# Head attention on one core: PSUM banks dealt out as two for the output and three fixed pairs, in place of one and a pool of seven

## The chip, the cores and the metric

The kernel runs on one core of a Trainium2 chip. The metric is the device time of one launch in microseconds (us); the three runs of the kernel before took 1464.88, 1465.10 and 1467.75 us, a median of 1465.1. TensorE has its own queue (PE, its weight loads shown as PEld), VectorE is DVE, ScalarE is ACT, GpSimd is POOL, and SP issues transfers. PSUM has eight banks of 128 partitions by 512 floats, and a matmul of 512 columns fills one bank.

## The reference, cut to what matters

One layer: layer norm, then a causal attention and a second attention with 16 heads over the same rows, then a routed feed-forward. The change lies in the second attention:

```python
attn = jnp.einsum('bhqd,bhkd->bhqk', q, k) / np.sqrt(DH)   # B=4, H=16, S=1024, DH=16
attn = jax.nn.softmax(attn, axis=-1)
sa = jnp.einsum('bhqk,bhkd->bhqd', attn, v)
```

The kernel takes the largest score of each query row first, subtracts it inside the score matmul, and lets ScalarE make the exponentials. The sums of the rows come out of the output matmul, whose values carry columns of ones.

## The kernel before, in words

The function `head_attention` works through 16 **steps** (4 batches by 4 groups of 4 heads). A step is cut into 16 **units**: two halves `c` of 512 queries, times eight blocks `j` of 128 keys. A unit has two **turns**, one for each pair of heads; I count turns through the whole stage as h = 0, 1, 2 and so on, so a step has 32 turns, unit u has the turns 2u (even) and 2u+1 (odd), and the last turn is 511. TensorE's program for one turn is, in this order:

- **scores** (`score`, L1687): two matmuls of 512 columns, one for each head of the pair, into the pair of banks `PAIR` of this turn; their increment `scored` releases ScalarE.
- **turned maxima** (`turn_maxima`, L1676), once a step: the finished maxima are transposed into one bank.
- **item** (`item`, L1668): two matmuls of 512 columns that compute scores again, of a later turn's step, for the maxima alone. They go into the pair of banks `SLOT`. The items run 40 turns ahead, so in the steady part each turn has one, and from turn 472 on there is none.
- **mix** (`mix`, L1708): half of the unit before's output matmuls, probabilities times values, 256 queries wide, added up in the bank `po` over the eight key blocks of a half `c`. The last block of a half `c` is not split: nothing in the even turn, all 512 columns in the odd turn.

ScalarE makes two exponentials for each scores pair (`fill`, L1768), in the order of the turns; `exp_done` counts them. Before the first exponential of a unit it also waits until the probabilities' buffer is free (`pv_done`). After four exponentials into the next half `c` it copies the finished output out of PSUM (`take_out`, L1775), which `out_taken` counts, and stores it. VectorE makes one reduction over both banks of an item (`maximum`, L1799); `sq_free` counts these and the readings of the turned maxima.

Each engine runs its own program in order, so a wait holds back all that stands behind it on the same engine. What TensorE waits for before it may write to a bank is worked out when the program is built: `Banks.give` notes who held each bank last, and `emptied` waits for all exponentials and reductions among these holders. The wait stands at the first weight load of the two matmuls and covers both banks. The banks come from the tables `PAIR_BANKS` and `SLOT_BANKS`, which repeat every seven turns. From the tables, and from the order of the program, follows for the steady part:

- scores of turn h wait, in five turns of seven, for the second exponential of turn h-2 and for the reduction of the item of turn h-2; in the sixth for that reduction alone, and in the seventh for the second exponential of turn h-2 and the first of turn h-1;
- the item of turn h waits, in five turns of seven, for the reduction of the item of turn h-2 and for the **first** exponential of turn h-1; in the sixth for the first exponential of turn h-1 alone, and in the seventh for the reduction of turn h-2 alone.

The output bank `po` is one. The first mix of a half `c` therefore waits for `take_out` of the half before:

```python
if j == 0:
    pe.wait_ge(out_taken, n * NQ + c)
```

In the last step (turns 480 to 511) there are no items; two of the seven banks then serve the first chunk of the feed-forward, and the scores go round the other five.

Of the kernel before, what the change touches and what calls it, by code (L numbers as in the profile page):

```python
# [6 lines left out]
F32 = mybir.dt.float32  # L7
BF16 = mybir.dt.bfloat16
F32R = mybir.dt.float32r
ACT = mybir.ActivationFunctionType  # L10
# [3 lines left out]
P = 128  # L14
B, S, D = 4, 1024, 256
N = B * S
CH = 512
# [6 lines left out]
VW = 2 * DH  # L24
# [25 lines left out]
DOTS = NT * DH  # L50
# [34 lines left out]
class HeadInputs:  # L85
# [3 lines left out]
    RING = 3  # L89
# [130 lines left out]
def project(nc, sem, x, w_kv_t, w_q, w_kc, w_vc, w_k, w_v, rope_cos, rope_sin,  # L220
# [7 lines left out]
    with ExitStack() as ctx:  # L228
# [25 lines left out]
        T, KA, VA, Q, KVC, K, V = range(7)  # L254
        BANKS = {T: 0, KVC: 1, KA: 2, VA: 3, Q: 0, K: 1, V: 2}

# [39 lines left out]
        with nc.Block() as block:  # L296
# [84 lines left out]
            def _(act):  # L381
# [11 lines left out]
                def take(it, s, j):  # L393

                    dst, src, stored = {
                        T: (xnT[s][:, :, :], ps[BANKS[T]][:, :, :], "xnT"),
                        KA: (kaT[s][:, :, :], ps[BANKS[KA]][:, :, :], "kaT"),
                        VA: (va[s][:, :, :].rearrange("p j d -> p (j d)"),
                             ps[BANKS[VA]][:, :, :].rearrange("p a b -> p (a b)"), "va"),
                        Q: (qk[:, 0:KD, :], ps[BANKS[Q]][:, :, :], None),  # L400
                        KVC: (kvc[s][:, :], ps[BANKS[KVC]][:, 0, :], None),
                        K: (qk[:, KD:2 * KD, :], ps[BANKS[K]][:, :, :], None),
# [1033 lines left out]
def head_attention(nc, inputs, ot_d, ffw, chunk, routing):  # L1436
# [3 lines left out]
    with ExitStack() as ctx:  # L1440
# [3 lines left out]
        RING = HeadInputs.RING  # L1444
# [3 lines left out]
        NQ = S // CH  # L1448
# [3 lines left out]
        PER = ITEMS // UNITS  # L1452
        PARTS = PAIRS
        assert PER == PARTS
        BANKS = 7
        LEAD = 4
        HELD = PER
        WARM = 8
# [4 lines left out]
        q6, k6, vh = inputs.q6, inputs.k6, inputs.vh  # L1463
        x1p = routing.parts_at(place)
        probs = [sb(f"h_p{i}", [P, GH, CH]) for i in range(PR)]
        outT = [sb(f"h_o{i}", [P, CH]) for i in range(NQ)]
# [4 lines left out]
        negm = room.take(TILES)  # L1471
        mparts = sb("h_mparts", [TILES, SHIFT, P], F32R)
        banks = ctx.enter_context(nc.psum_tensor("h_banks", [P, BANKS, CH], F32))
        po = ctx.enter_context(nc.psum_tensor("h_po", [P, CH], F32))

        const_set = sem("h_const_set")
        ones_set = sem("h_ones_set")
# [5 lines left out]
        out_taken = sem("h_out_taken")  # L1483
# [23 lines left out]
        def item_slot(n, m):  # L1507
            return n * ITEMS + m + max(0, n - 1 + (n >= 1 and m >= HELD))

        def turn_slot(n):  # L1510
            return (n + 1) * ITEMS + n + (HELD if n + 1 < STEPS else 0)

        LAST = STEPS - 1

        PAIR_BANKS = ((0, 1), (4, 0), (1, 2), (5, 6), (2, 3), (6, 0), (3, 4))
        SLOT_BANKS = ((2, 3), (5, 6), (3, 4), (0, 1), (4, 5), (1, 2), (5, 6))
        given = Banks()
        for slot in range(turn_slot(0) + LEAD * PER - HELD + 1):
            given.give(("SLOT", slot), *(SLOT_BANKS[3 + slot % 2] if slot != turn_slot(0) else (6,)))
        for h in range(LAST * UNITS * PARTS):  # L1520
            given.give(("PAIR", h), *PAIR_BANKS[h % BANKS])
            n, m = divmod(h + ITEMS + LEAD * PER, ITEMS)
            if m == HELD and n <= STEPS:
                given.give(("SLOT", turn_slot(n - 1)), PAIR_BANKS[(h + 1) % BANKS][0])
            if n < STEPS:
                given.give(("SLOT", item_slot(n, m)), *SLOT_BANKS[h % BANKS])
        given.give(("FIRST", 0), *OF_FIRST)
        for h in range(LAST * UNITS * PARTS, STEPS * UNITS * PARTS):
            given.give(("PAIR", h), *(b % OF_FIRST.start for b in (h * SIDES, h * SIDES + 1)))
# [5 lines left out]
        def bank_of(key, i=0):  # L1535
            return banks[:, given.places[key][i], :]
# [8 lines left out]
        with nc.Block() as block:  # L1545
# [105 lines left out]
            def _(pe):  # L1651
# [39 lines left out]
                def mix(n, w, part):  # L1691


                    c, j = divmod(w, QT)
                    u, last = n * UNITS + w, j == QT - 1 or n == LAST
                    if part == 0:
                        if j == 0:
                            pe.wait_ge(out_taken, n * NQ + c)
                        if w == 0 and n >= AHEAD:
                            pe.wait_ge(spread, n - AHEAD + 1)  # L1700
                        if last:
                            return
                    if part == 0 or last:
                        pe.wait_ge(exp_done, (u + 1) * GH)
                    at = slice(0, CH) if last else slice(part * CH // PARTS, (part + 1) * CH // PARTS)

                    for h in range(GH):
                        ins = nc.tensor.matmul(po[h * VW:(h + 1) * VW, at], vh[n % RING][:, j, h, :],  # L1708
                                               probs[u % PR][:, h, at], start=j == 0 and (part == 0 or last), stop=j == QT - 1)
                    if part == PARTS - 1:  # L1710
                        ins.then_inc(pv_done, 1)
# [12 lines left out]
                        routing.rank_tokens(pe, 0, first)  # L1724

                def keep_busy():
                    nc.tensor.matmul(po[:, :], q6[0][0:DOTS, 0, 0:P], k6[0][0:DOTS, 0, 0:CH], start=True, stop=True)

                for m in range(ITEMS):
                    item(0, m)  # L1730
                    if m >= ITEMS // 2:
                        keep_busy()
                for m in range(HELD):
                    item(1, m)
                    keep_busy()
                pe.wait_ge(const_set, 2)
                turn_maxima(0)
                for m in range(HELD, LEAD * PER):
                    item(1, m)
                    keep_busy()  # L1740
                for i in range(WARM):
                    nc.tensor.matmul(po[:, :], k6[1][:, 0, 0:P], k6[1][:, 0, 0:CH], start=True, stop=True)
                for u in range(STEPS * UNITS + 1):
                    n, w = divmod(u, UNITS)
                    ahead = [divmod(u * PER + ITEMS + LEAD * PER + b, ITEMS) for b in range(PER)]
# [15 lines left out]
            @block.scalar  # L1761
            def _(act):
                def fill(f):
                    u, h = divmod(f, GH)
                    if h == 0 and u >= PR:
                        act.wait_ge(pv_done, u - PR + 1)
                    act.wait_ge(scored, f // SIDES + 1)
                    nc.scalar.activation(probs[u % PR][:, h, :], bank_of(("PAIR", f // SIDES), f % SIDES), ACT.Exp,  # L1768
                                         scale=DH ** -0.5).then_inc(exp_done, 1)

                def take_out(n, c):
                    act.wait_ge(pv_done, n * UNITS + (c + 1) * QT)
                    if n:
                        act.wait_ge(stored[c], n * 16)
                    nc.scalar.activation(outT[c][:, :], po[:, :], ACT.Copy).then_inc(out_taken, 1)  # L1775

                def store(n, c):
                    act.wait_ge(out_taken, n * NQ + c + 1)
                    act.dma_start(ot_d[n, :, c * CH:(c + 1) * CH], outT[c][:, :]).then_inc(stored[c], 16)

                TAKE = GH
                HALF = QT * GH
                for f in range(STEPS * FILLS + TAKE + 1):
                    if f < STEPS * FILLS:
                        fill(f)
                    if f == LAST * FILLS + ROOT_AT * GH:
                        routing.root_by_log(act)
                    if f == LAST * FILLS + EXP_AT * GH:
                        routing.exponentials(act, 0)
                    if f >= HALF and (f - TAKE + 1) % HALF == 0:  # L1790
                        take_out(*divmod((f - TAKE + 1) // HALF - 1, NQ))
                    if f > HALF and (f - TAKE) % HALF == 0:
                        store(*divmod((f - TAKE) // HALF - 1, NQ))
# [541 lines left out]
def layer(nc, x, w_kv_t, w_q, w_kc, w_vc, w_k, w_v, w_o, ws_in, ws_out, w1, w2, w_g, w_e, b_g, b_e, n1_w, n2_w,  # L2335
# [16 lines left out]
    with ExitStack() as ctx:  # L2352
        heads = HeadInputs(nc, ctx, q_d, k_d, vh_d)
        with ExitStack() as first_stages:
            sem = first_stages.enter_context(stage_semaphores(nc))
            causal = CausalInputs(nc, first_stages, sem, xnT_d, kaT_d, va_d, tokens)
            turning = Turning(nc, first_stages, sem, heads, q_d, k_d)
            project(nc, sem, tokens, w_kv_t, w_q, w_kc, w_vc, w_k, w_v, rope_cos, rope_sin,
                    xn_d, xnT_d, kaT_d, va_d, vh_d, causal, turning)
            causal_attention(nc, sem, causal, xn_d, ya_d, heads, turning)  # L2360
        ffw = FeedForwardWeights(nc, ctx, w_o, ws_in, ws_out, w1, w2, w_g, w_e, b_g, b_e, n1_w, n2_w)
        chunk = Chunk(nc, ctx, ot_d, xn_d, rt_d)
        routing = Routing(nc, ctx, heads, ffw, chunk, idx_d)
        head_attention(nc, heads, ot_d, ffw, chunk, routing)
        feed_forward(nc, chunk, heads, ya_d, ffw, routing, rows_d, hidden_d, out.rearrange("b s d -> (b s) d"))
# [38 lines left out]
```

## Time and profile before

| | |
|---|---|
| median of three runs | 1465.1 us |
| the profiled execution | 1463.6 us |
| its span, first to last instruction | 1461.9 us |
| granted TensorE clock, mean over the span | 0.972 |
| TensorE matmul busy | 1380.3 us, 94% |
| VectorE busy | 1136.0 us, 78% |
| ScalarE busy | 854.8 us, 58% |
| reductions of items, L1799, 512 of them | 617.8 us, 1221 ns each |
| exponentials, L1768, 1024 of them | 551.2 us, 598 ns each |
| copies out, L1775, 32 of them | 598 ns each (median) |

The head attention's interleaved part runs from 345.5 us (first scores) to about 958 us (the start of the last step), and the last step to 1002 us. Shares of the whole span mix this with the stages around it, so the stage is read by its own stretches. A row of the timeline merges instructions of one line on one engine that follow each other; in brackets stands the idle time before them and what ended it. Matmuls are pipelined: the start of a weight load is a firmer mark than the end of a matmul.

### The profile page before, as it was taken

What the parts mean: (1) busy time and instruction counts of PE and PEld (TensorE: products, weight loads), DVE (VectorE), ACT (ScalarE), POOL (GpSimd) and SP (SyncE); (2) the same over time, 40 slices, a digit from 0 to 9 for tenths busy, and PEclk for the clock granted to TensorE, in tenths of its full rate; (3) what the DMA queues carried; (4) which work ended last, traced back from release to release, by engine and by line L of the source; (5) the groups of instructions that cost most, each with busy time, mean ns of one, the idle gap of its engine ahead of it and who ended that gap; (6) DMA issues with size and microseconds to landing.
All of it is one profiled execution on the core that took longest, in us unless ns stands there. A gap on an engine that the chain in (4) does not pass through costs nothing. (4 is left out here: it accounts for less than half of the span.)

```text
span 1461.9 us, 26960 instructions
## 1 busy us (share of the span) xinstructions
PE 1380.3 (94%) x9749; PEld 816.1 (56%) x9749; DVE 1136.0 (78%) x1803; ACT 854.8 (58%) x1573; POOL 371.9 (25%) x368
## 2 busy tenths in 40 slices
PE   6999799979999999999999999989999999989995
PEld 3655577734333333333333333335888888789985
DVE  3786575588999999999999999924677776657764
ACT  2445443304888888888888888885334343323332
POOL 0344294045241000000000000101233333355553
PEclk9999999957999999999999999999999999999998
DMA  5799769351443344443322234213565654365551
GB/s 188 266 320 342 250 224 249 71 98 59 91 109 67 44 67 66 67 67 60 67 55 51 46 58 67 75 59 47 166 161 153 175 152 132 88 217 177 176 174 62
DMA packets 119746, 185.06 MB, mean 127 GB/s; under 512 B 26614, under 2 KB 74122, under 8 KB 119622
## 3 DMA queue, kind: packets, MB, share of 16 engines
q1 hardware_dynamic: 94341, 124.55, 34.6%
q0 software_dynamic: 14816, 45.19, 10.4%
q10 hardware_dynamic: 10464, 13.64, 3.1%
q8 instruction: 82, 1.34, 0.4%
q14 instruction: 43, 0.34, 0.1%
HBM read 102.36 MB, written 81.88 MB: 126 GB/s over the span
## 5 line engine op out<-in xcount | busy, mean ns | idle before, releaser
L1799 DVE TENSOR_REDUCE i_saT<-h_banks 128x2 f32<-128x1024 f32 x512 | 617.8, 1221 | 24.9 <-PE h_banks L1668 17.1
L1768 ACT ACTIVATE h_p<-h_banks 128x512 f32<-128x512 f32 x1024 | 551.2, 598 | 137.3 <-PE h_banks L1687 121.9
L1708 PE MATMUL h_po<-h_p,h_v 128*32 128x256 f32 (+1 forms) x3728 | 318.4, 413 | 3.5 <-ACT h_p L1768 1.4
L1687 PE MATMUL h_banks<-h_q,h_k 50*128 50x512 f32 x1024 | 254.4, 495 | 11.7 <-ACT h_p L1768 6.0
L1668 PE MATMUL h_banks<-h_k,h_q 48*128 48x512 f32 x1024 | 222.8, 431 | 10.7 <-DVE i_saT L1799 6.8
L1687 PEld LDWEIGHTS h_banks<-h_q,h_k 50*128 50x128 f32 x1024 | 95.8, 183 | 235.0 <-ACT h_p L1768 190.4
L1708 PEld LDWEIGHTS h_po<-h_p,h_v 128*32 128x32 f32 x3728 | 73.4, 108 | 170.7 <-issue 83.8
L2130 PE MATMUL f_ob<-w_experts,f_h 128*128 x1032 | 146.4, 291 | 1.3 <-issue 0.2
L2130 PEld LDWEIGHTS f_ob<-w_experts,f_h 128*128 128x128 f32 x1032 | 129.9, 191 | 10.3 <-issue 8.1
L1564 POOL COPY h_v<-h_values 128x512 f32<-128x512 f32 x14 | 8.6, 612 | 459.4 <-DMA h_values<-vh_d 459.4
L1668 PEld LDWEIGHTS h_banks<-h_k,h_q 48*128 48x128 f32 x1024 | 101.1, 194 | 38.4 <-DVE i_saT L1799 28.0
L2176 ACT ACTIVATE h_v<-f_pair 128x512 f32<-128x512 f32 x64 | 38.2, 597 | 131.2 <-PE f_pair L2079 131.1
L2079 PE MATMUL f_pair<-w_routed,r_x1p 128*128 128x512 f32 x384 | 93.7, 400 | 2.1 <-PEq L70 2.1
L2079 PE MATMUL f_pair<-r_x1p,w_shared 128*128 128x512 f32 x384 | 92.9, 396 | 2.3 <-DVE f_rows L2238 2.3
L2079 PEld LDWEIGHTS f_pair<-w_routed,r_x1p 128*128 128x128 f32 x384 | 72.6, 191 | 18.3 <-issue 3.0
L2079 PEld LDWEIGHTS f_pair<-r_x1p,w_shared 128*128 128x128 f32 x384 | 71.3, 187 | 19.8 <-DVE f_rows L2238 3.1
L2238 DVE TENSOR_TENSOR h_place<-h_v,f_pair 128x512 f32<-128x512 f32 x48 | 32.9, 686 | 50.1 <-ACT h_v L2176 49.8
L746 PE MATMUL a_sc<-c_kT,c_qT 128*128 128x512 f32 (+3 forms) x192 | 68.3, 493 | 2.3 <-PEq L296 2.3
L1950 POOL TENSOR_TENSOR f_h<-h_place,f_h 128x512 fp32r<-128x512 f32 x32 | 43.8, 1368 | 98.6 <-ACT f_h L2169 97.0
L2251 DVE TENSOR_TENSOR f_h<-f_pair,f_h 128x512 fp32r<-128x512 f32 x43 | 29.7, 692 | 49.0 <-ACT f_h L2182 49.0
L308 POOL TENSOR_TENSOR h_spare<-h_spare,t_sin 128x512 f32<-128x512 f32 x28 | 41.9, 1530 | 101.3 <-DVE h_spare L184 101.3
L773 PE MATMUL a_out<-a_v,a_pT 128*128 128x256 f32 x432 | 63.6, 298 | 0.0
(266 smaller groups left out, 1695.5 us busy)
## 6 DMA issues: line engine op xcount, KB each, us to landing
h_q<-q_d SPq DMA_DIRECT2D x84, 128.0 KB, 5.9
h_k<-k_d SPq DMA_DIRECT2D x84, 128.0 KB, 7.0
ot_d<-h_o ACTq DMA_DIRECT2D x32, 256.0 KB, 2.9
q_d<-t_parts SPq DMA_DIRECT2D x12, 512.0 KB, 5.0
k_d<-t_parts SPq DMA_DIRECT2D x12, 512.0 KB, 5.1
p_xin<-in_L_attn_x SPq DMA_DIRECT2D x8, 512.0 KB, 5.1
xn_d<-p_xn SPq DMA_DIRECT2D x8, 512.0 KB, 5.1
xnT_d<-p_xnT SPq DMA_DIRECT2D x8, 512.0 KB, 6.0
```

The costliest lines, as they stand in the source:

```text
L308: last = nc.gpsimd.tensor_tensor(swap[:, j, :], swap[:, j, :], sin[:, s, :], ALU.mult)
L746: ins = nc.tensor.matmul(sc[u % 2][:, c:c + w], qT[b % 2][:, k, i * P:(i + 1) * P], kT[b % 2][:, k, c:c + w], start=k == 0, stop=k == KD - 1)
L773: ins = nc.tensor.matmul(out[u % 2][:, 0:D], pT[u % 2][left][:, j, :], vp[b % 2][right][:, j, :], start=j == 0 and n == 0, stop=j == i and ...
L1668: ins = nc.tensor.matmul(bank_of(("SLOT", slot), g), q6[r][at, p, i * P:(i + 1) * P], k6[r][at, p, half * CH:(half + 1) * CH], start=True, ...
L1687: ins = nc.tensor.matmul(bank_of(key, g), k6[r][at, p, j * P:(j + 1) * P], q6[r][at, p, c * CH:(c + 1) * CH], start=True, stop=True)
L1708: ins = nc.tensor.matmul(po[h * VW:(h + 1) * VW, at], vh[n % RING][:, j, h, :], probs[u % PR][:, h, at], start=j == 0 and (part == 0 or la ...
L1768: nc.scalar.activation(probs[u % PR][:, h, :], bank_of(("PAIR", f // SIDES), f % SIDES), ACT.Exp, scale=DH ** -0.5).then_inc(exp_done, 1)
L1799: nc.vector.tensor_reduce(halfmax[n % 2][:, m, :], both_banks(("SLOT", slot)), AX.X, ALU.max)\
L1950: nc.gpsimd.tensor_tensor(h[LO][:, i, :], whole[i % 2], h[HI][:, i, :].bitcast(F32), ALU.subtract).then_inc(h_split, 1)
L2079: ins = nc.tensor.matmul(ps[:, half, :], left, right, start=n == 0, stop=n == len(terms) - 1)
L2130: ins = nc.tensor.matmul(to, h[left][:, t % KH, k * P:(k + 1) * P], w2s[right][:, bass.ds(e, 1), k, :], start=k == 0 and n == 0, stop=k == ...
L2176: nc.scalar.activation(sil[f % 2], fills.buffer(key)[:, 0, :], ACT.Silu).then_inc(sil_done[f % 2], 1)
```

## The change

All eight banks are in use before and after; they are dealt out in another way.

- The output has two banks, `po[0]` and `po[1]`, which the halves `c` use by turns. The first mix of a half waits for the copy-out of the half before the last one.
- The pool for scores and items shrinks from seven banks to six, which are three fixed pairs: (0, 1), (4, 5), (2, 3). In turn h the scores take one pair and the item the next, in a round of three turns.
- The instructions on every engine and their order are as before; only the banks and the waits differ. The lines behind 1515 move down by one (L1668 becomes L1669, and so on).

From the new tables follows for the steady part: scores of turn h take the pair that the item of turn h-2 had, and wait for its reduction alone. The item of turn h takes the pair that the scores of turn h-1 had, and waits for **both** exponentials of turn h-1 and for nothing else. The turned maxima take a bank of the item before them and wait for its reduction. In the last step the scores go round four banks, and wait for both exponentials of turn h-2, where before they waited for the first of turn h-2 (and one of turn h-3).

```diff
-        BANKS = 7
+        BANKS = 6
...
-        po = ctx.enter_context(nc.psum_tensor("h_po", [P, CH], F32))
+        po = [ctx.enter_context(nc.psum_tensor(f"h_po{i}", [P, CH], F32)) for i in range(2)]
...
-        PAIR_BANKS = ((0, 1), (4, 0), (1, 2), (5, 6), (2, 3), (6, 0), (3, 4))
-        SLOT_BANKS = ((2, 3), (5, 6), (3, 4), (0, 1), (4, 5), (1, 2), (5, 6))
+        PAIR_BANKS = ((0, 1), (4, 5), (2, 3))
+        SLOT_BANKS = ((2, 3), (0, 1), (4, 5))
+        TURNS = len(PAIR_BANKS)
...
-            given.give(("PAIR", h), *PAIR_BANKS[h % BANKS])
+            given.give(("PAIR", h), *PAIR_BANKS[h % TURNS])
...
-                given.give(("SLOT", item_slot(n, m)), *SLOT_BANKS[h % BANKS])
+                given.give(("SLOT", item_slot(n, m)), *SLOT_BANKS[h % TURNS])
...
-                        if j == 0:
-                            pe.wait_ge(out_taken, n * NQ + c)
+                        if j == 0 and n * NQ + c >= 2:
+                            pe.wait_ge(out_taken, n * NQ + c - 1)
...
-                        ins = nc.tensor.matmul(po[h * VW:(h + 1) * VW, at], vh[n % RING][:, j, h, :],
+                        ins = nc.tensor.matmul(po[(n * NQ + c) % 2][h * VW:(h + 1) * VW, at], vh[n % RING][:, j, h, :],
...
-                    nc.scalar.activation(outT[c][:, :], po[:, :], ACT.Copy).then_inc(out_taken, 1)
+                    nc.scalar.activation(outT[c][:, :], po[(n * NQ + c) % 2][:, :], ACT.Copy).then_inc(out_taken, 1)
```

## Rows read from the trace of the kernel before

**Rows 1.** The page: the span, and the group of item reductions.

```profile
span 1461.9 us, 26960 instructions
L1799 DVE TENSOR_REDUCE i_saT<-h_banks 128x2 f32<-128x1024 f32 x512 | 617.8, 1221 | 24.9 <-PE h_banks L1668 17.1
```

**Rows 2.** Busy time by stretch (length, engines, granted clock, DMA): interleaved part, warm-up, last step.

```profile
345.50:958.00 612.50, 600.46 (x5514) 218.31 (x5515) 585.32 (x522) 532.66 (x989) 50.96 (x87) 1.00 0.37 65
320.00:340.00 20.00, 18.98 (x54) 8.47 (x52) 19.54 (x21) 0.00 (x0) 11.87 (x9) 0.50 0.17 55
...
970.00:975.00 5.00, 5.00 (x34) 1.22 (x32) 1.07 (x2) 4.98 (x11) 0.00 (x0) 1.00 0.26 92
995.00:1002.00 7.00, 5.95 (x44) 1.67 (x36) 3.57 (x19) 5.55 (x12) 0.00 (x0) 1.00 0.00 0
```

**Rows 3.** Timeline (start us, us, engine, line), steady turns from an even one at 720.52.

```profile
718.83 7.43 DVE L1799 TENSOR_REDUCE i_saT<-h_banks 128x2 f32<-128x1024 f32 x6
...
719.83 1.09 ACT L1768 ACTIVATE h_p<-h_banks 128x512 f32<-128x512 f32 x2
...
720.52 0.19 PEld L1687 LDWEIGHTS h_banks<-h_q,h_k 50*128 50x128 f32 x2 [0.41 <-ACT h_p L1768]
720.52 0.50 PE L1687 MATMUL h_banks<-h_q,h_k 50*128 50x512 f32 x2
720.63 0.19 PEld L1668 LDWEIGHTS h_banks<-h_k,h_q 48*128 48x128 f32 x2
...
721.13 2.28 ACT L1768 ACTIVATE h_p<-h_banks 128x512 f32<-128x512 f32 x4 [0.21 <-PE h_banks L1687]
...
721.19 0.16 PEld L1708 LDWEIGHTS h_po<-h_p,h_v 128*32 128x32 f32 x8 [0.37 <-ACT h_p L1768]
...
721.77 0.19 PEld L1687 LDWEIGHTS h_banks<-h_q,h_k 50*128 50x128 f32 x2 [0.43 <-ACT h_p L1768]
721.78 0.50 PE L1687 MATMUL h_banks<-h_q,h_k 50*128 50x512 f32 x2
721.88 0.19 PEld L1668 LDWEIGHTS h_banks<-h_k,h_q 48*128 48x128 f32 x2
...
723.01 0.19 PEld L1687 LDWEIGHTS h_banks<-h_q,h_k 50*128 50x128 f32 x2 [0.41 <-ACT h_p L1768]
...
725.49 0.19 PEld L1687 LDWEIGHTS h_banks<-h_q,h_k 50*128 50x128 f32 x2 [0.41 <-ACT h_p L1768]
```

**Rows 4.** Timeline of ACT alone, in two short windows (722.3 and 427.5 us).

```profile
722.32 1.09 ACT L1768 ACTIVATE h_p<-h_banks 128x512 f32<-128x512 f32 x2
...
427.54 0.60 ACT L1768 ACTIVATE h_p<-h_banks 128x512 f32<-128x512 f32 x1 [0.25 <-PE h_banks L1687]
```

**Rows 5.** Timeline where a half of the queries ends and the next begins.

```profile
426.92 0.22 PEld L1687 LDWEIGHTS h_banks<-h_q,h_k 50*128 50x128 f32 x2 [0.43 <-issue]
...
428.19 0.19 PEld L1668 LDWEIGHTS h_banks<-h_k,h_q 48*128 48x128 f32 x2 [0.19 <-ACT h_p L1768]
...
428.62 0.16 PEld L1708 LDWEIGHTS h_po<-h_p,h_v 128*32 128x32 f32 x8 [0.25 <-ACT h_p L1768]
...
429.62 0.19 PEld L1687 LDWEIGHTS h_banks<-h_q,h_k 50*128 50x128 f32 x2 [0.84 <-DVE i_saT L1799]
...
429.75 0.60 ACT L1775 ACTIVATE h_o<-h_po 128x512 f32<-128x512 f32 x1
...
430.40 0.16 PEld L1708 LDWEIGHTS h_po<-h_p,h_v 128*32 128x32 f32 x8 [0.49 <-ACT h_o L1775]
...
432.20 0.19 PEld L1687 LDWEIGHTS h_banks<-h_q,h_k 50*128 50x128 f32 x2 [0.41 <-ACT h_p L1768]
```

**Rows 6.** Timeline around turned maxima: the scores before and behind them, and their load.

```profile
459.66 0.19 PEld L1687 LDWEIGHTS h_banks<-h_q,h_k 50*128 50x128 f32 x2 [0.41 <-ACT h_p L1768]
...
460.17 0.10 PEld L1676 LDWEIGHTS h_banks<-i_saT 128*32 128x32 f32 x1 [0.33 <-issue]
...
461.40 0.18 PEld L1687 LDWEIGHTS h_banks<-h_q,h_k 50*128 50x128 f32 x2 [0.41 <-DVE h_mparts L1819]
```

More of the change, by code:

```diff
@@ L1513, in head_attention @@
         LAST = STEPS - 1
-        PAIR_BANKS = ((0, 1), (4, 0), (1, 2), (5, 6), (2, 3), (6, 0), (3, 4))
-        SLOT_BANKS = ((2, 3), (5, 6), (3, 4), (0, 1), (4, 5), (1, 2), (5, 6))
+        PAIR_BANKS = ((0, 1), (4, 5), (2, 3))
+        SLOT_BANKS = ((2, 3), (0, 1), (4, 5))
+        TURNS = len(PAIR_BANKS)
         given = Banks()
         for slot in range(turn_slot(0) + LEAD * PER - HELD + 1):
-            given.give(("SLOT", slot), *(SLOT_BANKS[3 + slot % 2] if slot != turn_slot(0) else (6,)))
+            given.give(("SLOT", slot), *(SLOT_BANKS[slot % 2 * 2] if slot != turn_slot(0) else (0,)))
         for h in range(LAST * UNITS * PARTS):
-            given.give(("PAIR", h), *PAIR_BANKS[h % BANKS])
+            given.give(("PAIR", h), *PAIR_BANKS[h % TURNS])
             n, m = divmod(h + ITEMS + LEAD * PER, ITEMS)
             if m == HELD and n <= STEPS:
-                given.give(("SLOT", turn_slot(n - 1)), PAIR_BANKS[(h + 1) % BANKS][0])
+                given.give(("SLOT", turn_slot(n - 1)), PAIR_BANKS[(h + 1) % TURNS][0])
             if n < STEPS:
-                given.give(("SLOT", item_slot(n, m)), *SLOT_BANKS[h % BANKS])
+                given.give(("SLOT", item_slot(n, m)), *SLOT_BANKS[h % TURNS])
         given.give(("FIRST", 0), *OF_FIRST)
@@ L1726, in keep_busy @@
                 def keep_busy():
-                    nc.tensor.matmul(po[:, :], q6[0][0:DOTS, 0, 0:P], k6[0][0:DOTS, 0, 0:CH], start=True, stop=True)
+                    nc.tensor.matmul(po[1][:, :], q6[0][0:DOTS, 0, 0:P], k6[0][0:DOTS, 0, 0:CH], start=True, stop=True)
                 for m in range(ITEMS):
@@ L1741, in _ @@
                 for i in range(WARM):
-                    nc.tensor.matmul(po[:, :], k6[1][:, 0, 0:P], k6[1][:, 0, 0:CH], start=True, stop=True)
+                    nc.tensor.matmul(po[1][:, :], k6[1][:, 0, 0:P], k6[1][:, 0, 0:CH], start=True, stop=True)
                 for u in range(STEPS * UNITS + 1):
```

## Prediction

> **What bounds the kernel now.** I read the page for the span (1461.9 us) [rows 1]; the profiled execution's own time is 1463.6 us, so 1.7 us lie around the span, and it stands 1.5 us under the median of 1465.1. Then I read the busy time by stretch. In the interleaved part, 345.5 to 958 us, TensorE is busy 600.46 of 612.50 us at a granted clock of 1.00, VectorE 585.32 and ScalarE 532.66 [rows 2]. TensorE and VectorE are both nearly full, so the timeline must tell which leads. Scores start at 720.52, 721.77, 723.01 and, two turns on, at 725.49 [rows 3]: 4.97 us for four turns, 1.24 a turn. Within a turn TensorE's steps follow without a hole: scores to mix 0.67 (720.52 to 721.19), mix to the next scores 0.58 (to 721.77) [rows 3]. VectorE makes six reductions in 7.43 us, 1.24 each [rows 3], and waits for items in only 17.1 us of the whole run [rows 1]. So it keeps step with TensorE and has next to nothing to give. A turn cannot become shorter than TensorE's 1.24 us, and any hole that recurs on TensorE lengthens the stage. ScalarE has room: two exponentials of a turn take 1.09 us [rows 3].
>
> **What the change takes away.** The first mix of a half of the queries waits for the copy-out. From scores to mix it is 0.78 us there (429.62 to 430.40, ended by L1775) against 0.67 in a steady turn [rows 3, 5]: a hole of 0.11 us. There are 32 halves; the first has nothing to wait for and the last one's mix is in the last step, so about 30 x 0.11 = 3.3 us are on TensorE's path. That is all that the second output bank can return. The copy-out itself, 0.60 us on ScalarE [rows 5], stays.
>
> The Trainium skill, page "Perfetto Trace Analysis", section "Optimizing Tensor Performance", asks that independent matmul groups rotate through PSUM banks, so that the evacuation of one overlaps the next group's matmuls. The hole at 430.40 is such an evacuation that doesn't overlap, so the trace agrees; by that rule alone the kernel would come out at about 1462.
>
> **What the change adds.** The item of turn h now needs the pair of banks that the scores of turn h-1 had, and so both exponentials of turn h-1. Before it needed the first. Look at the even turn at 720.52: its item starts to load at 720.63, but the two exponentials of the turn before run from 719.83 for 1.09 us, to 720.92 [rows 3]. So the new wait is 0.29 us too late at once, and in the next turn the item stands at 721.88 while the exponentials that began at 721.13 end near 722.22 (0.34 us). Behind the waiting item stand, on TensorE, the mix and the next scores; for these scores waits ScalarE. That closes a loop: exponentials of turn h, item of h+1, mix of h+1, scores of h+2, exponentials of h+2. It passes two turns, and its length is a sum of rows:
> - scores, load to end: 0.50 (720.52) [rows 3];
> - end of scores to the first exponential: 0.11 in even turns, where ScalarE has a second wait for the probabilities' buffer (721.02 to 721.13) [rows 3], and 0.04 in odd ones (722.28 to 722.32) [rows 3, 4];
> - both exponentials: 1.09 [rows 3, 4];
> - end of an exponential to the load of an item that waited for it: 0.05. One item in the trace shows it: the exponential ends at 427.54 + 0.60 = 428.14 and the load starts at 428.19 [rows 4, 5];
> - that item's load to the mix: 0.43 (428.19 to 428.62) [rows 5], since its weights can't load under the scores;
> - mix to the next scores: 0.57 (0.58 at 721.19; the item and the mix at 1.24 - 0.67) [rows 3].
>
> The loop of the even turns is 0.50 + 0.11 + 1.09 + 0.05 + 0.43 + 0.57 = 2.75 us, that of the odd turns 2.68. Two turns take 2.48 now. The longer loop sets the pace: the odd turn's scores then follow the even one's after 1.24, and the item of the odd turn waits some 0.4 us. The price is 2.75 - 2.48 = 0.27 us for two turns. If what separates the loops (ScalarE's second wait) cost nothing, it would be 0.20.
>
> Other loops stay shorter. Scores wait for the reduction of two turns ago; reduction (1.24), scores (0.50), exponentials (1.09 + 0.11), item (0.50, load to end as for scores) and handovers of about 0.05 make some 3.6 us for three turns, 1.20 a turn. VectorE gets its items later and idles.
>
> At the border of two halves the turn at 426.92 has no mix and the next one a mix of full width, with 1.00 us from mix to scores (428.62 to 429.62) [rows 5]. The two turns take 2.70 now (426.92 to 429.62); the loop gives 0.50 + 0.11 + 1.09 + 0.05 + 0.43 + 1.00 = 3.18, which is 0.48 more. The next two turns take 2.58 now (429.62 to 432.20), the hole of 0.11 included; the loop makes them 2.75, which is 0.17 more. So the hole is removed where the longer loop would cover it anyway, and the 3.3 us don't show.
>
> The turned maxima, once a step: scores to scores 1.74 there now (459.66 to 461.40) [rows 6]. Their bank now waits for the reduction of the item before, so they can't load as early as at 460.17; on the other side the loop is broken there and the next turn runs free. I take the 0.27 of any two turns, with 0.3 a step on either side.
>
> Sum for a step of 32 turns: 12 x 0.27 + 2 x 0.48 + 2 x 0.17 = 4.5 us. Fifteen steps: 68 us. The last four pairs of turns have no item, so 1 us less: 67. In the last step ScalarE is full (4.98 of 5.00 us) [rows 2], and the later scores wait (second exponential in place of the first of turn h-2) has a whole unit's exponentials to hide under; if that cover failed, it costs up to 0.1 us a unit, 1.6 us in all. I take 0. The warm-up's items use other pairs with the same two-deep turns: nothing. The stages before and behind are unchanged.
>
> So the profiled execution goes from 1463.6 to about 1530.6, and the median, 1.5 above, to about 1532; I say 1531.
>
> **Rivals.** (1) *The wait is met in time.* Then only the copy-out's hole goes: 1465.1 - 3.3 = 1462, faster. It needs the second exponential to end before the item's load, 0.29 us earlier than at 720.92; ScalarE's slack would allow that only if scores came earlier, and they stand behind item and mix on the same queue. Against it speak the rows themselves. Chance 0.03. (2) *Nothing moves*, because the loop closes inside 2.48: one of my handovers would have to be 0.27 too long, while all but 0.05 of the sum is read directly. Chance 0.04, 1465. (3) *The clock falls.* New holes of some 0.3 us recur on TensorE, busy then about 0.90 of the time. In 995 to 1002 us it was busy 5.95 of 7.00 us, 0.85, at a clock of 1.00 [rows 2], which speaks against it; in 320 to 340 us the clock was 0.50, that is 1.2 GHz [rows 2]. If a tenth of the stage ran so, TensorE's 1.24 a turn would double in 48 turns: 60 us more, about 1590. Chance 0.05.
>
> The page "TensorE: Matmul & The Clock Gate" of the Trainium skill, section "A second HAM failure mode: psum-queue depth-cycling", tells of a kernel whose matmuls cycled through PSUM banks with small idle times between groups, and whose clock went to and fro between its levels. That rule speaks for rival 3; the row of 995 to 1002 us doesn't bear it out here.
>
> **How the numbers follow.** My forecast has 0.88. Its own ends: low, 0.20 for two turns: (12 x 0.20 + 2 x 0.41 + 2 x 0.10) x 15 - 1 = 50 us, 1515; high, the maxima at double price and ScalarE's copy-out pushing the exponentials behind it by 0.1 to 0.2 at each border: 67 + 4 + 6 + 1.6 = 79 us, 1544. With some room, 1512 to 1546, which leaves out the three rivals (0.12) and a little of my own case. About 0.2% (3 us) is what a measurement here tells from no change: faster 0.03, same 0.04, slower 0.93.
>
> **What would show it.** Right: scores start alternately 1.24 and about 1.51 us apart; item loads (L1669) appear as waiting for the exponentials (L1769) in nearly every odd turn, with some 0.3 us of idle weight path before each; VectorE's idle time before reductions rises from 17 to about 80 us; nobody waits for L1776; the clock in the stage stays 1.00. Wrong: the scores 1.24 apart throughout (rivals 1, 2), a clock under 1.00 between 345 and 1000 us (rival 3), or a growth that sits in the last step or at the turned maxima alone.

## The result and the profile after

The changed kernel takes 1544.3 us in the median of 4 runs (1537.1 to 1550.2), against 1466.2 for the kernel before. The ratio is 1.052, with a 95% interval of 1.049 to 1.055. The forecast of 1531 had the direction and the mechanism, and was 13 us short. One execution of the kernel before taken beside the later runs ran in a slower state (1542.8 us at a mean clock of 0.83) and counts in no median or ratio below. The profiled execution went from 1463.6 to 1544.7 us, its span from 1461.9 to 1543.0, so 81.1 us are to be found.

The page first (its groups: busy us, mean ns, idle us before and what ended it; then the granted clock and TensorE in 40 slices):

```profile
span 1543.0 us, 26313 instructions
L1800 DVE TENSOR_REDUCE i_saT<-h_banks 128x2 f32<-128x1024 f32 x512 | 621.4, 1222 | 89.9 <-PE h_banks L1669 83.2
L1669 PEld LDWEIGHTS h_banks<-h_k,h_q 48*128 48x128 f32 x1024 | 101.5, 194 | 122.0 <-ACT h_p L1769 84.9
PEclk9999999856999999999999999999999999999998
PE   6999898889999999999999999998999999989995
```

VectorE's work is unchanged (621.4 us against 617.8), but it now waits 83.2 us for items where it waited 17.1 [rows 1]. The weight loads of the items (L1669) sat idle 84.9 us until an exponential (L1769) ended. The waits of 350 to 1036 us (us, times, longest) say how often:

```profile
PEld h_banks L1669 <- ACT h_p L1769: 84.9, 239, 1.1
DVE i_saT L1800 <- PE h_banks L1669: 78.6, 239, 3.2
```

That is about one item in two. The busy time by stretch (start:end, length, then busy us of PE, PEld, DVE, ACT, POOL, granted clock, DMA) is that of the interleaved part, to be read beside [rows 2], and then of a piece near its start and of the last step:

```profile
350.30:1036.00 685.70, 662.03 (x5514) 244.93 (x5513) 588.95 (x522) 532.08 (x989) 50.98 (x87) 0.99 0.33 58
354.00:374.00 20.00, 20.00 (x118) 6.43 (x112) 11.73 (x10) 9.77 (x19) 9.11 (x7) 0.50 0.27 78
1035.72:1082.44 46.72, 40.71 (x248) 14.92 (x244) 15.56 (x57) 37.33 (x74) 3.41 (x2) 0.93 0.13 44
```

The same 5514 matmuls and 522 operations of VectorE take 685.7 us in place of 612.5. Nothing was added; for the most part the engines wait for each other. The second row is what the sum did not have: 20 us just behind the start in which the granted clock is 0.50, that is 1.2 GHz.

By stage, from the starts of the scores in both traces: ahead of the first scores +4.8 us, first scores to the last step +73.1, last step +2.5, behind it +0.7. In the nine other profiles, all with the same code ahead of it, the first item starts between 295.4 and 303.2 us, so the 4.8 is a spread of executions and no effect of the change.

The steady turns of the changed kernel (timeline: start us, us, engine, line; in brackets the idle time and what ended it):

```profile
735.12 2.26 ACT L1769 ACTIVATE h_p<-h_banks 128x512 f32<-128x512 f32 x4 [0.49 <-PE h_banks L1688]
735.75 0.19 PEld L1688 LDWEIGHTS h_banks<-h_q,h_k 50*128 50x128 f32 x2 [0.41 <-DVE i_saT L1800]
736.25 0.19 PEld L1669 LDWEIGHTS h_banks<-h_k,h_q 48*128 48x128 f32 x2 [0.32 <-ACT h_p L1769]
736.68 0.16 PEld L1709 LDWEIGHTS h_po<-h_p,h_v 128*32 128x32 f32 x8 [0.24 <-issue]
737.25 0.19 PEld L1688 LDWEIGHTS h_banks<-h_q,h_k 50*128 50x128 f32 x2 [0.41 <-issue]
737.86 2.26 ACT L1769 ACTIVATE h_p<-h_banks 128x512 f32<-128x512 f32 x4 [0.48 <-PE h_banks L1688]
738.50 0.19 PEld L1688 LDWEIGHTS h_banks<-h_q,h_k 50*128 50x128 f32 x2 [0.41 <-DVE i_saT L1800]
739.00 0.19 PEld L1669 LDWEIGHTS h_banks<-h_k,h_q 48*128 48x128 f32 x2 [0.31 <-ACT h_p L1769]
```

Scores start at 735.75, 737.25 and 738.50: 1.50 and 1.25 us apart, 2.75 for two turns. The loop can be walked in these rows. Scores at 737.25, exponentials at 737.86 (0.61 later, which is 0.50 + 0.11). The row at 737.86 merges four exponentials; the second of them by itself:

```profile
738.35 0.59 ACT L1769 ACTIVATE h_p<-h_banks 128x512 f32<-128x512 f32 x1
```

It ends at 738.94, 1.08 behind 737.86, and the item loads at 739.00 (0.06). One pair earlier, item to mix is 0.43 (736.25 to 736.68) and mix to scores 0.57 (to 737.25). Every term is within 0.01 us of the one that the prediction took.

### The profile page after: what moved, and what is told of

Its sections match the earlier page's. It is cut to its first block and busy times, and to the rows that moved or that the text cites. A ratio compares the mean times of both kernels' runs of the same rounds, so it can differ in the third digit from the quotient of the medians.

```text
span 1543.0 us, 26313 instructions
## 1 busy us (share of the span) xinstructions
PE 1444.3 (94%) x9749; PEld 842.3 (55%) x9749; DVE 1141.6 (74%) x1803; ACT 854.3 (55%) x1573; POOL 371.1 (24%) x368
## 5 line engine op out<-in xcount | busy, mean ns | idle before, releaser
L1800 DVE TENSOR_REDUCE i_saT<-h_banks 128x2 f32<-128x1024 f32 x512 | 621.4, 1222 | 89.9 <-PE h_banks L1669 83.2
L1769 ACT ACTIVATE h_p<-h_banks 128x512 f32<-128x512 f32 x1024 | 551.0, 597 | 199.8 <-PE h_banks L1688 186.5
L1709 PE MATMUL h_po<-h_p,h_v 128*32 128x256 f32 (+1 forms) x3728 | 323.5, 419 | 1.4 <-ACT h_p L1769 1.4
L1669 PE MATMUL h_banks<-h_k,h_q 48*128 48x512 f32 x1024 | 248.3, 481 | 25.8 <-ACT h_p L1769 12.6
L1688 PE MATMUL h_banks<-h_q,h_k 50*128 50x512 f32 x1024 | 257.8, 502 | 7.1 <-ACT h_p L1769 4.5
L1669 PEld LDWEIGHTS h_banks<-h_k,h_q 48*128 48x128 f32 x1024 | 101.5, 194 | 122.0 <-ACT h_p L1769 84.9
```

The costliest lines, as they stand in the source:

```text
L1669: ins = nc.tensor.matmul(bank_of(("SLOT", slot), g), q6[r][at, p, i * P:(i + 1) * P], k6[r][at, p, half * CH:(half + 1) * CH], start=True, ...
L1688: ins = nc.tensor.matmul(bank_of(key, g), k6[r][at, p, j * P:(j + 1) * P], q6[r][at, p, c * CH:(c + 1) * CH], start=True, stop=True)
L1709: ins = nc.tensor.matmul(po[(n * NQ + c) % 2][h * VW:(h + 1) * VW, at], vh[n % RING][:, j, h, :], probs[u % PR][:, h, at], start=j == 0 an ...
L1800: nc.vector.tensor_reduce(halfmax[n % 2][:, m, :], both_banks(("SLOT", slot)), AX.X, ALU.max)\
```

## The experiments

The times of each kernel below the first two rows were taken beside runs of the kernel before on the same chip (a median of 1464.4 us for wait_both, one_output, swap_waits and half_exp, 1466.7 for the other four). The table holds what the traces gave: distances from scores to scores over two turns in the sixth of the 16 steps, and the lengths of step 0 and of a usual step.

| kernel | median us (range) | ratio, 95% | steady pair | border pair, the next | maxima pair | step 0 | usual step |
|---|---|---|---|---|---|---|---|
| before | 1466.2 (1464.9 to 1467.8) | 1 | 2.47 | 2.67, 2.58 | 2.96 | 40.3 | 40.8 |
| after | 1544.3 (1537.1 to 1550.2) | 1.052 (1.049 to 1.055) | 2.74 | 3.16, 2.79 | 3.33 | 52.0 | 45.4 |
| wait_both | 1530.0 (1525.4 to 1540.8) | 1.047 (1.041 to 1.052) | 2.74 | 3.16, 2.79 | 2.86 | 46.9 | 44.9 |
| one_output | 1536.6 (1532.3 to 1547.4) | 1.050 (1.044 to 1.056) | 2.74 | 3.16, 2.79 | 3.34 | 44.5 | 45.4 |
| swap_waits | 1521.6 (1515.4 to 1533.1) | 1.037 (1.033 to 1.041) | 2.69 | 3.10, 2.78 | 3.34 | 57.6 | 44.6 |
| half_exp | 1485.2 (1484.5 to 1492.2) | 1.015 (1.011 to 1.020) | 2.53 | 2.96, 2.57 | 3.33 | 42.0 | 42.2 |
| both_half | 1475.0 (1466.1 to 1485.0) | 1.005 (1.003 to 1.008) | 2.46 | 2.73, 2.57 | 3.39 | 49.6 | 41.2 |
| half_exp_before | 1460.1 (1458.5 to 1463.9) | 0.995 (0.993 to 0.998) | 2.47 | 2.67, 2.58 | 2.88 | 40.2 | 40.7 |
| after_again | 1539.1 (1532.9 to 1550.6) | 1.049 (1.045 to 1.053) | 2.74 | 3.17, 2.79 | 3.34 | 60.4 | 45.4 |
| fill_start | 1535.4 (1533.1 to 1537.7) | 1.046 (1.044 to 1.048) | 2.74 | 3.16, 2.79 | 3.33 | 44.6 | 45.4 |

**The wait alone, on the old banks.** The kernel before, with its seven banks and its one output bank, and the item of turn h made to wait for both exponentials of turn h-1.

```diff
-                def emptied(key):
+                def emptied(key, exps=0):
...
-                    if pairs:
-                        pe.wait_ge(exp_done, max(h * SIDES + g + 1 for h, g in pairs))
+                    exps = max([exps] + [h * SIDES + g + 1 for h, g in pairs])
+                    if exps:
+                        pe.wait_ge(exp_done, exps)
...
-                    emptied(("SLOT", slot))
+                    emptied(("SLOT", slot), max(0, n * ITEMS + m - ITEMS - LEAD * PER) * SIDES)
```

> The kernel before, its seven banks and its one output bank untouched; only each item now also waits for both exponentials of the turn before. If the loop of exponentials, item, mix and scores sets the pace, two turns take 2.75 us in place of 2.48 and the kernel takes 1530 to 1548 us, as the changed one. If it is the smaller pool (scores that wait for reductions, banks in fixed pairs), nothing of it is here: 1464 to 1470.

Measured: 1530.0 us, 65.6 above the kernel before. The steady turns of this kernel, timeline:

```profile
738.95 0.19 PEld L1688 LDWEIGHTS h_banks<-h_q,h_k 50*128 50x128 f32 x2 [0.41 <-issue]
739.55 2.28 ACT L1769 ACTIVATE h_p<-h_banks 128x512 f32<-128x512 f32 x4 [0.40 <-PE h_banks L1688]
740.20 0.19 PEld L1688 LDWEIGHTS h_banks<-h_q,h_k 50*128 50x128 f32 x2 [0.41 <-ACT h_p L1769]
740.68 0.18 PEld L1669 LDWEIGHTS h_banks<-h_k,h_q 48*128 48x128 f32 x2 [0.30 <-ACT h_p L1769]
```

Scores to scores 1.25, exponentials 0.60 behind scores, the item at 740.68 behind two exponentials that end near 740.64: the same 2.74 for a pair and the same 3.16 and 2.79 at the borders, with no new banks at all. The later exponential in the item's wait is enough to make most of the loss, 65.6 of the 72.2 us that one_output, with the changed kernel's six banks, loses on the same chip; which banks lie where isn't needed for that. One figure differs: the pair with the turned maxima is 2.86 here and 3.33 in the changed kernel; in the mean of steps 1 to 13 it is 2.95 against 3.34, and 0.4 us in each of 15 steps is 6 of the other 7 us. So that part comes from the banks (below).

**One output bank.** The changed kernel with the second output bank taken back and everything else kept.

```diff
-        po = [ctx.enter_context(nc.psum_tensor(f"h_po{i}", [P, CH], F32)) for i in range(2)]
+        po = [ctx.enter_context(nc.psum_tensor(f"h_po{i}", [P, CH], F32)) for i in range(1)]
...
-                        if j == 0 and n * NQ + c >= 2:
-                            pe.wait_ge(out_taken, n * NQ + c - 1)
+                        if j == 0:
+                            pe.wait_ge(out_taken, n * NQ + c)
...
-                        ins = nc.tensor.matmul(po[(n * NQ + c) % 2][h * VW:(h + 1) * VW, at], vh[n % RING][:, j, h, :],
+                        ins = nc.tensor.matmul(po[0][h * VW:(h + 1) * VW, at], vh[n % RING][:, j, h, :],
...
-                    nc.scalar.activation(outT[c][:, :], po[(n * NQ + c) % 2][:, :], ACT.Copy).then_inc(out_taken, 1)
+                    nc.scalar.activation(outT[c][:, :], po[0][:, :], ACT.Copy).then_inc(out_taken, 1)
```

> The changed kernel with one output bank again (the eighth bank lies idle). If the longer loop covers the copy-out's hole, the second output bank returns nothing: within 3 us of the changed kernel, and the pair of turns behind a border of two halves stays at 2.79 us. If the second bank works for itself, that pair is 0.11 us longer at each of 30 borders: 3.3 us slower than the changed kernel.

Measured: 1536.6 us, inside the spread of the changed kernel's ten executions (1532.9 to 1550.6; medians 1544.3 and, in after_again, 1539.1). That spread is wider than the 3.3 us in question, so the traces have to tell. Who waited for what, from the rows on the output's tile, first of the changed kernel:

```profile
  PEld h_po L1709: 0.2, 1
```

and then of this one:

```profile
  PEld h_po L1709: 14.5, 30
```

The loads of the mix wait for the copy-out (L1776) 30 times again, as before the change, and the pair of turns in which they do it is as long with the wait as without (2.79 both times). The second bank removes the wait, and these pairs are no shorter for it.

**The waits of ScalarE in the other order.** The loop of the even turns is longer than that of the odd ones by ScalarE's second wait (0.11 against 0.04). Here ScalarE waits for the scores first and then for the probabilities' buffer, which has long been free.

```diff
+                    act.wait_ge(scored, f // SIDES + 1)
                     if h == 0 and u >= PR:
                         act.wait_ge(pv_done, u - PR + 1)
-                    act.wait_ge(scored, f // SIDES + 1)
```

> The changed kernel; ScalarE's two waits before the first exponential of a unit change places (scores first, then the probabilities' buffer). If the loop of the even turns sets the pace and its 0.11 us from scores to exponential is the way the second wait is passed, it falls to the 0.04 us of the odd turns: 2.68 us for two turns, 0.06 less in 16 pairs of 15 steps, 12 to 15 us faster than the changed kernel. If another loop or a bank sets the pace, or both waits cost the same in either order, no difference beyond 3 us.

Measured: the pair goes from 2.74 to 2.69 and a step from 45.4 to 44.6, 0.8 x 15 = 12 us; the median is 15.0 us under that of one_output on the same chip. Timeline of this kernel:

```profile
737.82 0.19 PEld L1688 LDWEIGHTS h_banks<-h_q,h_k 50*128 50x128 f32 x2 [0.41 <-issue]
738.37 2.31 ACT L1769 ACTIVATE h_p<-h_banks 128x512 f32<-128x512 f32 x4 [0.38 <-PE h_banks L1688]
739.05 0.19 PEld L1688 LDWEIGHTS h_banks<-h_q,h_k 50*128 50x128 f32 x2 [0.41 <-DVE i_saT L1800]
739.50 0.19 PEld L1669 LDWEIGHTS h_banks<-h_k,h_q 48*128 48x128 f32 x2 [0.27 <-ACT h_p L1769]
740.51 0.19 PEld L1688 LDWEIGHTS h_banks<-h_q,h_k 50*128 50x128 f32 x2 [0.41 <-issue]
```

Scores to exponentials is 0.55 (737.82 to 738.37) in place of 0.61, and 737.82 to 740.51 is 2.69. A saving of 0.06 on ScalarE, an engine that the changed kernel keeps busy for 532 of 686 us, shows at once in the pair: it lies on the loop.

**Shorter exponentials, by doses.** In half_exp the second exponential of each turn covers 256 of its 512 columns from the third unit on; in both_half both do. A quarter of the probabilities (half_exp) or half of them (both_half) are thus not computed, so these kernels do less work on ScalarE; their times serve only to weigh the loop. half_exp_before does the same as half_exp to the kernel before.

```diff
-                    nc.scalar.activation(probs[u % PR][:, h, :], bank_of(("PAIR", f // SIDES), f % SIDES), ACT.Exp,
-                                         scale=DH ** -0.5).then_inc(exp_done, 1)
+                    wide = CH // 2 if u >= PR and f % SIDES else CH
+                    nc.scalar.activation(probs[u % PR][:, h, 0:wide], bank_of(("PAIR", f // SIDES), f % SIDES)[:, 0:wide],
+                                         ACT.Exp, scale=DH ** -0.5).then_inc(exp_done, 1)
```

and for both_half

```diff
+                    wide = CH // 2 if u >= PR else CH
```

> The changed kernel, but from the third unit on the second exponential of each turn covers 256 of its 512 columns, so half of those probabilities are stale. If the loop sets the pace, it shortens by about the 0.2 us that 256 columns take, to some 2.54 us for two turns, and the kernel falls to 1480 to 1495 us. If the pace is set by reductions or banks, which don't see this, it stays at 1535 to 1550.

> The changed kernel, but from the third unit on both exponentials of a turn cover 256 of their 512 columns, so half of the probabilities are stale. The loop then falls to about 2.53 - 0.22 = 2.31 us, under the 2.48 that TensorE needs by itself. If the loop alone made the kernel slower, two steady turns take 2.48 us again and the kernel comes to 1464 to 1476 us (the turned maxima, 3.33 in place of 2.97 us once a step, stay). If the pool of three pairs has a second limit near 2.74 (reductions), it stays over 1500.

> The kernel before with the second exponential of each turn at 256 of 512 columns from the third unit on (half of those probabilities stale). TensorE sets its pace, so by the theory the steady turns stay at 1.24 us and the time within 4 us of the kernel before: a shorter exponential is worth something only where an item waits for it. If exponentials were a limit in any kernel of this family, it would become some 20 us faster.

Measured, half_exp, 1485.2 us, timeline:

```profile
737.76 0.18 PEld L1688 LDWEIGHTS h_banks<-h_q,h_k 50*128 50x128 f32 x2 [0.41 <-DVE i_saT L1801]
738.31 0.87 ACT L1770 ACTIVATE h_p<-h_banks 128x512 f32<-128x512 f32 x2 [0.30 <-PE h_banks L1688]
739.23 0.19 PEld L1669 LDWEIGHTS h_banks<-h_k,h_q 48*128 48x128 f32 x2
740.29 0.19 PEld L1688 LDWEIGHTS h_banks<-h_q,h_k 50*128 50x128 f32 x2 [0.41 <-DVE i_saT L1801]
```

The two exponentials take 0.87 in place of 1.09, 0.22 less, and the pair 2.53 (737.76 to 740.29) in place of 2.74, 0.21 less. With both halved the loop is under TensorE's own 2.48 and the pair stops there, at 2.45 to 2.47 (1475.0 us). In the kernel before, half_exp's cut of ScalarE's work leaves the steady pair at 2.47: there ScalarE isn't on the path. It still gains 6.6 us in the median, more than the 4 us allowed for. Of the 3.5 us that its profiled execution is shorter, 2.9 lie in the last step (44.2 to 41.3), where ScalarE is the full engine [rows 2], and 1.6 in the interleaved part, with 1 us lost elsewhere. The other 3.1 us are what the profiled execution of the kernel before (1463.6) stands under the median of 1466.7.

The trace of both_half also suggests why the second output bank returns nothing even where the loop no longer binds. Its next pair behind a border is 2.57, against 2.58 before. Timeline of a steady turn's exponentials and of a border:

```profile
556.28 0.66 ACT L1770 ACTIVATE h_p<-h_banks 128x256 f32<-128x256 f32 x2 [0.52 <-PE h_banks L1688]
...
562.33 0.60 ACT L1777 ACTIVATE h_o<-h_po 128x512 f32<-128x512 f32 x1 [0.84 <-PE h_po L1709]
562.84 0.16 PEld L1709 LDWEIGHTS h_po<-h_p,h_v 128*32 128x32 f32 x8 [0.36 <-issue]
562.95 0.33 ACTq L1781 DMA_DIRECT2D ot_d<-h_o  x1
563.33 0.38 ACT L1770 ACTIVATE h_p<-h_banks 128x256 f32<-128x256 f32 x1
563.76 0.19 PEld L1669 LDWEIGHTS h_banks<-h_k,h_q 48*128 48x128 f32 x2 [0.16 <-ACT h_p L1770]
```

The mix at 562.84 starts while the copy-out still runs (to 562.93), so the hole of [rows 5] is gone. But the copy-out stands ahead of the two exponentials on ScalarE, and the issue of the output's store (L1781, 0.33) between them, so that they end 0.89 us behind the start of the first (562.82 to 563.71) and not 0.66. The item at 563.76 waits for the second of them. In this kernel the hole has moved by one instruction on TensorE's queue; no run takes the copy-out or the store away.

**The changed kernel once more, and with its start filled.** after_again is the changed kernel itself. In fill_start two matmuls that nobody reads stand ahead of the items of turns 1 and 2, the first that wait.

```diff
                         if coming[0] < STEPS:
+                            if u * PARTS + part in (1, 2):
+                                keep_busy()
+                                keep_busy()
                             item(*coming)
```

> The changed kernel once more, unchanged. If the granted clock falls back behind the first scores in some executions and not in others, its times spread over 10 us or more, the slow ones with the lower mean clock, and the first step's length in the profile lies between 44.5 and 58 us while the other steps stay at 45.4. If the low clock belonged to this kernel firmly, the first step is 52 us again and the times lie within 4 us.

> The changed kernel with two idle matmuls (into the second output bank, which nobody uses yet) ahead of the items of the second and third turn, where TensorE would stand still and wait for exponentials. If the fall of the clock comes from that standstill, the first step takes 44.5 to 45.5 us, the times lie close to the lowest of the changed kernel (about 1535) and within 5 us. If the fall has another cause, the first step and the spread are as without them.

Measured: the same pairs in every steady turn, but step 0 takes 60.4 us in after_again, more than the 58 that was allowed for, and 44.6 in fill_start. The difference is the clock. Busy time by stretch, of after_again:

```profile
352.00:390.00 38.00, 37.61 (x203) 12.12 (x203) 21.11 (x18) 19.20 (x36) 15.86 (x11) 0.50 0.16 49
```

of fill_start, the whole of step 0:

```profile
352.16:396.79 44.63, 43.37 (x366) 17.06 (x366) 38.82 (x35) 34.80 (x65) 18.21 (x13) 1.00 0.20 54
```

and the second us behind the first scores, first of the changed kernel, then of the kernel before:

```profile
351.33:352.33 1.00, 0.32 (x2) 0.19 (x2) 1.00 (x1) 1.00 (x4) 0.71 (x1) 1.00 0.00 0
```

```profile
346.48:347.48 1.00, 0.73 (x4) 0.30 (x4) 1.00 (x2) 0.90 (x3) 0.72 (x1) 1.00 0.00 0
```

In the first turns there is no mix yet. The scores of turn 1 start 0.34 us behind those of turn 0 (1.20 in the kernel before, where they waited for an exponential themselves), and then the item of turn 1 stands until both exponentials of turn 0 are done:

```profile
352.01 0.19 PEld L1669 LDWEIGHTS h_banks<-h_k,h_q 48*128 48x128 f32 x2 [1.15 <-ACT h_p L1769]
```

So TensorE does 0.32 us of work in that us where it did 0.73. Some 3 us behind the first scores the granted clock falls to 0.50 in this execution, and two turns take 4.32 us until it rises again. This happened in the profiles of after (353.5 to 373 us), wait_both, swap_waits, both_half and after_again, and not in those of one_output, half_exp and fill_start, of which one_output has the same first turns as the changed kernel. So it is a matter of the single execution. The profiles differ in when the clock had risen. In after, swap_waits, both_half and after_again it was at 1.00 throughout the first us behind the first scores, and fell for 20 us or more. In one_output it rose during that us and stayed up, though the second us is as empty (its first two us, granted clock 0.86 and 1.00):

```profile
353.21:354.21 1.00, 1.00 (x7) 0.60 (x6) 0.10 (x1) 0.33 (x1) 0.73 (x1) 0.86 0.00 0
354.21:355.21 1.00, 0.30 (x4) 0.18 (x2) 1.00 (x1) 1.00 (x3) 0.77 (x1) 1.00 0.00 0
```

half_exp (0.50 in the first us) stayed up too. wait_both (0.79, and never under 0.62 us of work) fell for 7 us all the same, so an empty us by itself doesn't tell which execution falls. With the start filled the five times lie within 4.7 us (1533.1 to 1537.7), without it the six on the same chip within 17.8 (1532.9 to 1550.6). The mean granted clock of a run tells which: in after_again 1550.6 us goes with 0.956 and 1532.9 with 0.972. The link from the standstill to the fall rests on these five times, all at a mean clock of 0.968 to 0.971. The profile of fill_start can't carry it, since its clock rose as late as that of one_output (0.78 in the first us), which kept it without the filling. The link is likely, and not shown beyond that.

No kernel here that does all the work comes under the one before. The best with the later wait is swap_waits at 1521.6.

## Why the prediction was right, and where it was short

**The loop** was right in each term, and in its sum: 2.75 was worked out, 2.74 measured; 3.18 and 3.16 at the border, 2.75 and 2.79 behind it. wait_both makes it from the wait alone, swap_waits and half_exp shorten the loop by what its terms lose, and both_half finds the floor of 2.48 that the prediction named.

**The sum for a step** was 4.5 us. In steps 1 to 13 the mean step goes from 40.83 to 45.43, 4.60. By their means over these steps, the steady pairs grew by 0.27 as taken, the border pairs by 0.46 (0.48 was taken), those behind them by 0.20 (0.17) and the pair with the maxima by 0.31 (0.27; 0.37 in the sixth step), so no term is off by more than 0.04. The maxima's pair doesn't follow the loop, as half_exp and both_half leave it at 3.33 and 3.39. The prediction's other reason applies, the bank that waits for the reduction of the item before; the waits of 345 to 1000 us show it, 14 times 0.41:

```profile
PE h_banks L1677 <- DVE i_saT L1800: 5.8, 14, 0.4
```

**The interleaved part** as a whole was to grow by 67 us and grew by 73.1 in the profile. Step 0 took 52.0 us, where the two profiles of the same turns at full clock, one_output and fill_start, took 44.5 and 44.6. So about 7.4 us are the clock, and 65.7 the longer waits: 4.3 in step 0, 59.8 in steps 1 to 13 and 1.6 in step 14, where four pairs of the kernel before were already 0.2 to 0.6 us longer than usual. On the chip where it was tried, fill_start stands 68.7 us above the kernel before, against 67 in the sum; this is the change without the fall.

**The step that failed** is rival 3, set aside at 0.05 as a thing of the whole stage, on the evidence of 995 to 1002 us [rows 2]. Where it was looked for, it didn't come: the waits of 0.3 us in every pair leave the clock at 1.00 (fill_start's step 0 above). They are idle time of the weight loads; the matmuls fill 43.37 of 44.63 us by their records, 0.97, where the prediction had worked out 0.90. The fall came where the prediction didn't look, behind the first two turns, whose item wait has no mix beside it. By the prediction's own sign, a clock under 1.00 between 345 and 1000 us, it did come in this execution, for 20 us of 686. The price is nothing in some executions and up to about 16 us in others (60.4 against 44.6), not 60; a turn at 0.50 takes 2.16 us, not twice 1.24. The text let the wait stand as one more 0.27 there too.

The rule of the Trainium skill that was weighed for it, "TensorE: Matmul & The Clock Gate", section "A second HAM failure mode: psum-queue depth-cycling", speaks of idle times that recur between groups. The trace doesn't bear it out here: with recurring waits the clock stays at 1.00. The fall at the start of the stage stands behind a single standstill, which is another case.

**The last step** was taken at nothing, with up to 1.6 us if the cover failed. It grew by 2.5 in this profile (44.2 to 46.7), and by 1.3 and 1.4 in fill_start and one_output (45.5 and 45.6). The cover did fail: typical pairs go from 1.66 and 2.05 to 1.74 and 2.40 with the four banks, while wait_both, which keeps the old banks there, has 1.66 and 2.05 in places. The rest of the 2.5 is put down to the clock, which also dips in that step of the kernel before; its granted mean was 0.93 here, and 0.96 in one_output.

**The copy-out's hole** was worth up to 3.3 us if nothing covered it; the prediction gave it nothing, and one_output agrees. The trace of both_half adds that the loop's cover is not the only reason: with the copy-out and the store's issue among the exponentials on ScalarE, the pair behind a border stays at 2.57 even there.

**The median** rose by 78.1 us (1466.2 to 1544.3). Of that 68.7 remain when the start is filled, 1.7 more than the sum. The other 9.4 us are put down to the clock at the start, across two sets of runs; beside fill_start on one chip the changed kernel was 3.7 us above fill_start in the median and 15.2 at most. Which executions fall stays open. In the profile 14.1 us were missed (1530.6 to 1544.7): 7.4 of the clock, 4.8 ahead of the stage, 2.5 in the last step and 0.7 behind it, less 1.3 of the longer waits (65.7 for 67). That 1544.3 still lies under the 1546 of the range is luck in part: the top of the range was made of the maxima at twice their price, the copy-out and the last step, while most of the miss came from the clock and from the spread ahead of the stage.

## What to carry to other kernels

When all eight PSUM banks are in use, a bank given to one stream is a bank taken from another; write down for each matmul the last reader of its bank before and after the change, and close the loop from there. If the loop reaches back to the same matmul n turns later, its length divided by n is the least time of a turn, and it can be summed from a trace of the kernel before, here to within 0.01 us (2.75 against 2.74). Look at the first turns of a stage by themselves, since the work that hides a wait in the steady state may not be there yet.

## What the runs showed of the hardware

- With a wait of about 0.3 us before an item's weight loads in each 2.74 us, the granted clock stayed at 1.00 through the 45 us of step 0 (fill_start). In the four profiles with the clock at 1.00 from the first scores on and 0.31 to 0.32 us of matmul in the us behind the first, it fell to 0.50, for 20 us in one (after) and at least 38 in another (after_again); one_output, with 0.30 us in that us and 0.86 in the first, kept it.
- The order of two waits ahead of an exponential costs 0.06 us when the one that ends last is placed second: 0.61 us from scores to exponential against 0.55 the other way round.
- Half the columns take off less than half of an exponential's time: two of 512 columns take 1.09 us, one of 512 and one of 256 0.87, two of 256 0.66 (both_half), so 0.22 us for 256 columns.
